# Thirty matmuls of zeros ahead of four layers of a graph network, in two groups around TensorE's first transposes

## What is computed

```
for l in range(5):
    edge_fea = concat([edge_attr[:, 3:] @ ew1[l], edge_attr[:, 0:3] @ ew2[l]], -1)
    msg = norm[:, None] * (h[row] + edge_fea)
    agg = segment_sum(msg, col, num_segments=n)
    h = relu(concat([h, agg], 1) @ mlp_w[l] + mlp_b[l])
    h = (h - h.mean(0)) * rsqrt(h.var(0) + eps) * bn_g[l] + bn_b[l]
    if l != 4: h = relu(h)
```

## Time and profile before

| | us |
|---|---|
| median of 3 runs (1693.99 to 1695.84) | 1694.28 |
| span of the profiled execution, first to last instruction | 1693.0 |
| TensorE busy (86% of the span) | 1461.4 |
| line 654, 3500 matmuls | 698.8 |
| line 735, 560 matmuls | 242.2 |
| line 644, 200 transposes of layers 2 to 5 | 40.9 |
| VectorE, ScalarE, GpSimd busy | 675.2, 387.6, 166.6 |

### The profile page before, as it was taken

The page is one execution under the profiler, slowest core; times in us unless marked ns, Lnnn a source line. Parts: engine busy times, 40 slices in busy tenths (PEclk is TensorE's granted clock), DMA queues, the critical chain, the costliest instruction groups (busy, mean ns, idle before and its releaser), DMA issues.

```text
span 1693.0 us, 24943 instructions
## 1 busy us (share of the span) xinstructions
PE 1461.4 (86%) x8538; PEld 814.1 (48%) x8539; DVE 675.2 (40%) x1560; ACT 387.6 (23%) x1010; POOL 166.6 (10%) x145
## 2 busy tenths in 40 slices
PE   3564678888889899989999899998999873999996
PEld 2553444444443444535444454534445443566664
DVE  7989777777621220122201230112201357233332
ACT  1220443434401400023001320014000330233332
POOL 1000000000000000000000000000000003466664
PEclk9875899999989999989999899999999876899999
DMA  5153000000000000000000000000004090233433
GB/s 134 38 195 108 1 1 1 1 2 1 14 2 0 14 1 0 1 15 1 0 1 0 14 1 1 1 0 13 1 0 95 7 334 20 52 63 63 66 64 40
DMA packets 49549, 57.87 MB, mean 34 GB/s; under 512 B 14319, under 2 KB 41601, under 8 KB 49184
## 3 DMA queue, kind: packets, MB, share of 16 engines
q1 hardware_dynamic: 38688, 41.67, 8.6%
q0 software_dynamic: 10752, 14.69, 5.4%
HBM read 42.36 MB, written 13.99 MB: 33 GB/s over the span
## 4 chain that ended last, share of the span: by engine, by line
PE 76%; DVE 12%; ACT 5%; issue 4%; DVEq 2%; DMA 1%; POOL 1%; SPq 0%; POOLq 0%; ACTq 0%
PE bank L654 37%; PE bank L735 13%; PE bank L1148 6%; PE bank L1163 6%; ACT at L1618 3%; PE bank L1752 3%; PE bank L1154 1%; PE bank L644 1%; DVE ohL L1409 1%; PE bank L1697 1%; PE bank L738 1%; PE bank L1750 1%; PE bank L1140 1%; DVE ohS L1524 1%; DVEq L505 1%
## 5 line engine op out<-in xcount | busy, mean ns | idle before, releaser
L654 PE MATMUL bank<-at,m 125*128 125x500 fp8e4 (+1 forms) x3500 | 698.8, 356 | 9.4 <-issue 3.1
L654 PEld LDWEIGHTS bank<-at,m 125*128 125x128 f16 x3500 | 319.0, 98 | 345.9 <-issue 39.0
L663 DVE TENSOR_TENSOR aggT<-bank,dinvB 128x500 f32<-128x500 f32 (+1 forms) x70 | 42.2, 620 | 345.8 <-PE bank L654 345.8
L826 ACT ACTIVATE hT<-bank,prm 128x500 f32<-128x500 f32 (+1 forms) x70 | 40.5, 630 | 602.8 <-PE bank L738 602.8
L874 POOL TENSOR_TENSOR idJ<-idJ,wts 125x1400 f32<-125x1400 f32 x2 | 8.0, 4005 | 1406.0 <-DVE idJ L1032 1406.0
L735 PE MATMUL bank<-hT,wcur 128*128 128x500 f32 (+1 forms) x280 | 125.3, 570 | 0.0
L788 DVE BATCH_NORM_STATS2 zst<-hT 128x6 f32<-128x500 f32 (+1 forms) x70 | 40.3, 617 | 199.9 <-ACT hT L826 199.9
L735 PE MATMUL bank<-aggT,wcur 128*128 128x500 f32 (+1 forms) x280 | 116.9, 540 | 0.0
L1148 PE MATMUL bank<-w1s,xtT 128*128 x224 | 109.3, 611 | 0.1
L1163 PE MATMUL bank<-w2s,h1T 128*128 x448 | 106.1, 380 | 1.4 <-ACT h1T L939 1.4
L623 DVE SCALAR_TENSOR_TENSOR m<-bank,dinvP,m 125x256 f16<-125x256 f32 x100 | 48.0, 483 | 148.2 <-ACT m L635 148.2
(11 more groups left out here) (319 smaller groups left out, 1446.7 us busy)
## 6 DMA issues: line engine op xcount, KB each, us to landing
slrow<-sl_dram SPq DMA_DIRECT2D x26, 512.0 KB, 4.8
w1s<-in_L_ffn_W SPq DMA_DIRECT2D x1, 4096.0 KB, 14.2
w2s<-in_L_ffn_W SPq DMA_DIRECT2D x1, 4096.0 KB, 18.9
xin<-in_x SPq DMA_DIRECT2D x1, 2800.0 KB
x<-in_x SPq DMA_DIRECT2D x1, 2800.0 KB
out_rows<-x SPq DMA_DIRECT2D x1, 2800.0 KB
xn_dram<-xn SPq DMA_DIRECT2D x1, 2800.0 KB
wraw<-in_L_gnn_mlp_w SPq DMA_DIRECT2D x5, 512.0 KB, 3.6
```

Source lines behind the costliest of these rows:

```text
L654: last = pe.matmul(bank[banks[g % len(banks)]][:, 0:w], m[:, s, k, h * 128:(h + 1) * 128], at_block(g // H)[:, s, :], start=s == 0 and k = ...
L663: dve.tensor_tensor(aggT[:, h, a:a + w], bank[banks[g % len(banks)]][:, 0:w], dinvB[:, a:a + w], ALU.mult).then_inc(s_agge, 1)
```

## The change

In layers 2 to 5, on the way that is taken, TensorE multiplies zeros: 22 matmuls of 500 columns ahead of the first transposes, and 8 more between the transposes of tile 2 and the first matmuls of tile 0. All write bank 7, whose next use begins a fresh sum (`start=True`); nothing reads them, and they wait for no semaphore. `zeros` is a bf16 tile of 128 x 128, `nought(CQ)` its first column repeated 500 times, so each is one weight load and one matmul.

```
+        BUSY = (22, 8)
+
+        def keep_busy(pe, n):
+
+            for _ in range(n):
+                pe.matmul(bank[7][:, 0:CQ], zeros[:, 0:128], nought(CQ), start=True, stop=True)
+
         def aggregate_pe(pe, base, prev, l):
...
             with pe.If(gathers == 0):
                 behind = 2
+                keep_busy(pe, BUSY[0])
                 for t in range(NT + behind):
                     if t < NT:
                         row_pe(pe, base, prev, t)
+                    if t == behind:
+                        keep_busy(pe, BUSY[1])
                     if t >= behind:
                         pe.wait_ge(s_lo, base(NT) + t - behind + 1)
```

## The result

| | median us | lowest to highest |
|---|---|---|
| before (10 runs) | 1694.92 | 1690.24 to 1699.78 |
| after (10 runs) | 1700.77 | 1698.28 to 1706.56 |

The ratio is 1.0039 with a 95% interval of 1.0025 to 1.0053: 6.6 us slower, between 4.2 and 9.0. The forecast was 1702.0, and 1696.0 to 1705.5.

The account below looks back on a forecast made before the run. TensorE, holding 76% of the chain of waits, was taken to bound the kernel. Layers 3 and 4 lose 5.9 + 3.8, layers 2 and 5 gain 2.0: 7.7 on the 1693.0 span, 1700.7, plus 1.3 gives 1702.0 us; range 1696.0 to 1705.5.

Parts of the forecast that it names:

- The reading of the branch: Layers 3 and 4: the flag's branch frees TensorE's sequencer only 4.8 us into a 5.6 us pause, so zeros start late.
- Layers 2 and 5: Zeros start at once after the linear stage and keep the clock high; gains of 1.5 and 0.55 us, together 2.0.
- The sub-step that layer 2's 22 would end with 0.9 us to spare: Layer 2's pause: the 22 zeros take 4.64 us and end at 558.4, 0.9 us before the pause ends.
- The wait for code after the sixth zero: Layers 3 and 4: TensorE stops for code behind the sixth zero, idle 1.8 and 1.0 us.
- The clock: Layer 3: back 3.8 us into the sixteen zeros, 5.9 us late; layer 4: return counted from first zeros, 3.8 late.
- My late bound: Layer 4: 5.5 us late if the clock's return is counted from 956.85 instead of from the first zeros.
- The sum: Whole kernel: 5.9 + 3.8 - 2.0 = 7.7 us slower on the span of 1693.0, giving 1700.7.
- the first (no wait for code): Layers 3 and 4: code comes in time, 2.9 and 3.3 us late; kernel +4.2 us, 1698.5; chance 0.27.
- the second: Layers 3 and 4: clock back after 1.9 us, no code wait; kernel +2.3 us, 1696.6; chance 0.12.
- the third: Layers 3 and 4: far branch over before the linear stage ends, all pauses filled; 7.4 us faster, 1686.9; chance 0.08.
- The fourth (zeros don't hold the clock): Layers 2 to 5: all 30 zeros run cold wherever the clock has fallen; kernel +28.3 us, 1722.6; chance 0.05.
- The price of 0.8 us for the second group: Before the first dense tile: the 8 zeros cost 0.8 us over a warm start without them.

Follow-up runs that it names:

- loop_only: Changed kernel with the zeros of layers 2 to 4 only, layer 5 as before the change; median 1703.91 us, ratio to before 1.0067.
- ahead_of_branch: Changed kernel, loop kept, with the 22 zeros moved ahead of the flag's read and branch, the 8 staying; 1696.96 us, ratio to before 1.0022.
- written_out_zeros: Changed kernel (22 and 8 zeros) with TensorE's loop over layers 2 to 4 written out; 1688.94 us, ratio to before 0.9972.
- written_out_22_0: Changed kernel with TensorE's loop written out, 22 zeros ahead of the transposes and no second group; 1686.20 us, ratio to before 0.9944.
- written_out_0_8: Changed kernel with TensorE's loop written out, no first group, only the 8 zeros before the first dense tile; 1700.96 us, ratio to before 1.0035.
- written_out_alone: Kernel before with TensorE's loop over layers 2 to 4 written out, no zeros; 1692.78 us, ratio to before 0.9992.
- written_out_25_0: Changed kernel with TensorE's loop written out, 25 zeros ahead of the transposes and no second group; 1686.67 us, ratio to before 0.9951.
- written_out_25_3: Changed kernel with TensorE's loop written out, 25 zeros ahead of the transposes and 3 behind the third pair; 1687.51 us, ratio to before 0.9960.
- written_out_11_0: Changed kernel with TensorE's loop written out, 11 zeros ahead of the transposes and no second group; 1692.51 us, ratio to before 0.9984.

## Why the prediction was right, and in which terms it was not

**The reading of the branch** was right and carried the sign. The far branch took 2.40 and 2.76 us in layers 3 and 4 and the zeros started 4.2 and 5.0 us into the pause (5.0 and 4.8 forecast). The transposes started 6.7 and 9.2 us later than ScalarE was ready, the second just outside the 4 to 9 named.

**Layers 2 and 5**: 1.4 and 0.4 us gained (1.5 and 0.55). The sub-step that layer 2's 22 would end with 0.9 us to spare was wrong: there too TensorE stopped for code behind the sixth, and the zeros ended just as ScalarE was ready. It cost nothing, by luck of 0.2 us: in loop_only the same stop was 0.90 us, and the transposes of layer 2 started 0.15 later.

**The wait for code after the sixth zero** was right in place in both layers, and of a different size: 0.56 and 1.66 us idle (1.8 and 1.0 forecast). I had taken over the times at which the code came before. From the end of the branch to the seventh zero it was 3.4 us in layer 3 and 4.5 in layer 4, where before it had been 4.5 and 3.8 to the first dense matmul; that time isn't fixed. The place was given as 256 instructions behind the loop's head. Counted in the program, it is the branch's target that stands 255 behind the head; the seventh zero stands at 268. The stop in ahead_of_branch is at 13, 255 instructions before that; so the two stops are about one block apart.

**The clock**: in layer 3 it came back 3.2 us after the sixteen had begun (3.8 forecast), and that layer lost 3.8, not 5.9. In layer 4 I had the return counted from the first zero, at the cost of only one cold matmul; it came 4.2 us after the break and 8.5 after the first zero, and the layer lost 6.7, not 3.8. My late bound for it, 5.5, was too small as well. The two errors nearly cancel, 10.5 against 9.7 for the two layers together: that the sum came out so close is luck; the sign and the order of size are not.

**The sum** was 7.7 on the span, and 8.7 in the heads of the profiled run; over all runs 6.6.

**Rivals**: the first (no wait for code) is not what happened, though its 4.2 lies at the low end of the interval; the second is out, as the clock came back after 3.2 and 4.2 us and not 1.9; the third needed a branch that is over before the linear stage ends, and written_out_zeros shows that its mechanism is real: with the near branch the change is faster than before. The fourth (zeros don't hold the clock) is refuted by PEclk 1.00 in the heads of layers 2 and 5. The price of 0.8 us for the second group was right, but that it "isn't needed for the clock", as the expectation for written_out_22_0 had it, was wrong in one layer of four.

The Trainium skill ("Runtime: NRT & Kernel Launch", "Instruction fetch mechanics") was the page that bore on this: code in blocks, and a wait at a branch that leaves those at hand. The traces agree: in layers 3 and 4 the branch takes 2.2 to 5.0 us in each of the kernels with the loop, and 0.2 to 0.4 in all layers of those without it. In layer 3 of the changed kernel a block of code arrives between 753.0 and 754.1 us, while TensorE's sequencer stands at that branch (753.1 to 755.5).

## What to carry to other kernels

In these kernels, filling a pause to hold TensorE's clock paid only where the filler could start when the pause began and was done about when the real work was ready; look at the sequencer's rows (jumps, branches, waits by "issue") before you look at the engine's. A filler that starts after the clock has fallen runs at half the pace, in order, ahead of the real work: in the heads, eight such matmuls cost 7.4 us (written_out_0_8 against written_out_alone), more than the 5.1 that twenty-two early ones gain (written_out_22_0); by the ratios the two are alike, 7.3 and 8.1. And count both ends: 11 held nothing, 22 three layers of four, 25 all four (26 would fill the 5.5 us, at 0.211 each).

## What the runs showed of the hardware that I had not expected

- Zeros of bf16, with a column repeated by a stride of nothing as the moving side, keep TensorE at 2.4 GHz: PEclk 1.00 in all heads of written_out_zeros, written_out_25_0 and written_out_25_3.
- The clock fell 2.1 to 4.8 us after the engine's last work in unfilled pauses of 4.2 to 5.7 us. It can fall behind a pause too: in layers 3 and 5 of written_out_11_0 it fell 0.1 and 0.5 us after the transposes had begun. Once, in layer 3 of written_out_22_0, it fell although no pause was longer than 0.95 us: two pauses, 0.95 and 0.74, with three pairs of transposes between them. In that case at least, the pause wasn't whole; whether the transposes count for less than other matmuls wasn't tested.
- A branch over some 250 instructions, counted in the program, took 0.2 to 0.4 us, or 2.2 to 5.0 us in the turns that the sequencer had come back to from the loop's end; the jump back itself took 3.3 to 3.8. For the same code the idle time ahead of the next block was 0.56 us in one turn of the loop and 1.66 in the next. Where a stop for code ended, the matmul behind it started 1.3 to 1.6 us after a block had come in.
- Moving the filler ahead of the branch, on a path that runs anyway, made the branch itself longer by 2.3 and 2.5 us (5.0 and 4.9 against 2.7 and 2.4 before, in layers 3 and 4).
